# Weights of three key tiles made on VectorE in a cross-attention kernel, lane by lane, and self-attention sums in two banks

## The reference

```python
x = x + _L0_attn_ref(_layernorm(x), L0_attn_Wqvk, L0_attn_Wo)
x = x + _L0_xattn_ref(_layernorm(x), ctx_768, Wq, bq, Wk, bk, Wv, bv, Wo, bo)
x = x + _L0_ffn_ref(_layernorm(x), router_w, router_b, W1, b1, W2, b2)
# cross attention: 16 heads of 8 channels, scale 8 ** -0.5
attn = softmax(einsum('bhqd,bhkd->bhqk', q, k) * scale)
x = einsum('bhqk,bhkd->bqhd', attn, v).reshape(B, Nq, Cq) @ Wo + bo
```

## Time and profile before

| | |
|---|---|
| time, median of three runs | 1010.72 us |
| profiled execution, time | 1012.52 us |
| its span, first to last instruction | 1010.6 us |
| TensorE matmul busy | 878.2 us (87%), 6128 |
| ScalarE busy | 868.4 us (86%), 664 |
| VectorE busy | 178.0 us (18%), 537 |
| mean granted TensorE clock | 0.976 of 2.4 GHz |
| L696, exponentials, ScalarE | 784.3 us, 520 |
| L1341, sums of cross attention | 422.6 us, 3200 matmul records |
| L1311, scores | 266.1 us, 1792 matmul records |

### The profile page before, as it was taken

How to read it: one execution, slowest core, us unless ns; L and a number is a source line. 1 busy time by engine, 2 the same in 40 slices (tenths; PEclk the granted TensorE clock), 3 DMA queues, 4 the chain that set the end, 5 groups by cost and what they waited for, 6 DMA issues and landing times.

```text
span 1010.6 us, 14927 instructions
## 1 busy us (share of the span) xinstructions
PE 878.2 (87%) x6128; PEld 257.8 (26%) x6128; DVE 178.0 (18%) x537; ACT 868.4 (86%) x664; POOL 8.6 (1%) x33
## 2 busy tenths in 40 slices
PE   6978888999888888888899888888888888899997
PEld 4552222222111111111112211111111111134443
DVE  6755644320000000000003000000000000043212
ACT  4656888999999999999999999999999999943332
POOL 3000000000000000000000000000000000000000
PEclk9985999999999999999999999999998999999999
DMA  4251006511112111111221111111221000020200
GB/s 142 105 188 38 1 2 117 182 32 32 35 38 51 43 34 32 32 35 34 42 55 33 36 32 35 35 32 41 41 46 35 3 1 1 1 85 1 84 11 10
DMA packets 19717, 46.32 MB, mean 46 GB/s; under 512 B 6210, under 2 KB 9388, under 8 KB 19132
## 3 DMA queue, kind: packets, MB, share of 16 engines
q1 hardware_dynamic: 19644, 45.31, 17.9%
HBM read 38.18 MB, written 7.11 MB: 45 GB/s over the span
## 4 chain that ended last, share of the span: by engine, by line
PE 34%; issue 31%; ACT 31%; DVE 3%; DMA 0%; ACTq 0%; DVEq 0%
ACT probs L696 31%; PE psum L1341 10%; PE psum L1311 6%; PE psum L1561 5%; PE psum L1573 5%; PE psum L1210 1%; PE psum L1244 1%; PE psum L1458 1%; DVE turned L914 1%; PE psum L1248 1%; PE psum L1337 1%; PE psum L1231 0%; PE psum L1444 0%; PE psum L1194 0%; DVE xn L787 0%
## 5 line engine op out<-in xcount | busy, mean ns | idle before, releaser
L696 ACT ACTIVATE probs<-psum 128x1536 f32<-128x1536 f32 (+1 forms) x520 | 784.3, 1777 | 36.9 <-PE psum L1311 24.6
L1341 PE MATMUL psum<-probs,v_ctx 128*9 128x512 f32 x3200 | 422.6, 600 | 3.1 <-DVE turned L914 2.7
L1311 PE MATMUL psum<-q_all,k_ring 32*128 32x512 f32 (+1 forms) x1792 | 266.1, 496 | 106.1 <-ACT probs L696 100.4
L1311 PEld LDWEIGHTS psum<-q_all,k_ring 32*128 32x128 f32 x1792 | 103.7, 186 | 503.1 <-ACT probs L696 452.1
L914 DVE STREAM_TRANSPOSE turned<-psum 128x512 f32<-128x512 f32 x16 | 11.5, 717 | 626.2 <-PE psum L1337 609.0
L748 ACT ACTIVATE probs<-psum,b_sb 128x512 f32<-128x512 f32 x64 | 44.0, 687 | 71.9 <-PE psum L1561 71.8
L1341 PEld LDWEIGHTS psum<-probs,v_ctx 128*9 128x9 f32 x3200 | 47.6, 88 | 104.7 <-issue 97.7
L1561 PE MATMUL psum<-xnT,w_region 128*128 128x512 f32 x128 | 65.3, 594 | 1.9 <-issue 1.9
L1573 PE MATMUL psum<-probs,ctx_region 128*128 128x512 f32 x128 | 65.0, 592 | 0.0
L1341 PE MATMUL psum<-probs,v_self 128*9 128x512 f32 (+3 forms) x384 | 43.3, 553 | 2.9 <-DVE turned L914 1.7
L1573 PEld LDWEIGHTS psum<-probs,ctx_region 128*128 128x128 f32 x128 | 24.3, 190 | 30.6 <-issue 30.6
(11 more groups left out here) (144 smaller groups left out, 251.3 us busy)
## 6 DMA issues: line engine op xcount, KB each, us to landing
k_ring<-kc_parts SPq DMA_DIRECT2D x256, 52.0 KB
k_ring<-kc_parts SPq DMA_DIRECT2D x256, 48.0 KB
kc_parts<-kparts_bc SPq DMA_DIRECT2D x8, 512.0 KB, 2.8
probs<-gate_rows SPq DMA_DIRECT2D x4, 1024.0 KB, 6.0
kc_parts<-probs SPq DMA_DIRECT2D x4, 512.0 KB, 2.8
w_region<-in_L_ffn_W SPq DMA_DIRECT2D x1, 2048.0 KB, 13.3
ctx_region<-in_ctx SPq DMA_DIRECT2D x1, 768.0 KB, 7.8
ctx_region<-in_ctx SPq DMA_DIRECT2D x1, 672.0 KB, 6.3
```

The source lines that it names most:

```text
L696: act.activation(probs[:, slot:slot + w, :], psum[:, at:at + w, :], ACT.Exp, scale=SC[ph]).then_inc(L[ph]["exp_done"], 1)
L1311: mm = pe.matmul(into[:, col:col + n_q], keys, q_all[rows, g, hf * HALF + q0:hf * HALF + q0 + n_q], start=True, stop=True)
L1341: mm = pe.matmul(into[:, q0:q0 + w], v_all[:, h, t, :], probs[:, place(ph, at)[1], col:col + w], start=first, stop=last)
```

## The change

**A plan with tiles for VectorE.** In units 1, 2, 3, 5, 6 and 7 the tiles 0, 13 and 26 are taken out of ScalarE's list. Their banks (four lanes each, 72 in all) are laid one at a time into bank 3 of every other group of four, beside three of ScalarE's, as soon as ScalarE's list has reached that tile. In unit 1 the lanes of tile 0 stand in groups 67, 71, 75 and 79, those of tile 13 in 83, 87, 91 and 95, those of tile 26 in 99, 103, 107 and 111; the other units have the same spacing. The number of groups is unchanged. The batch of such a tile comes `VECTOR_LAG` = 6 groups behind its last lane: that of tile 0 in turn 85.

**What VectorE does for a lane.** The queries are scaled so that the scores are in powers of two (ScalarE's exponential multiplies with ln 2). VectorE rounds to the nearest integer, takes the rest, builds the power of two from the integer's bits and multiplies it with a polynomial of the rest: eight instructions, each waiting for the one before. The factor in front of the polynomial is multiplied into a copy of the values of the three tiles (`vector_v`, three more instructions before cross attention). The weights lie in four buffers, one per lane, in the space of `v_self` and `w_quads`. TensorE waits before it scores into a bank for the first two of the eight (`taken`), and before a batch for the last (`made`).

**Self attention.** The first half's sums alternate between banks 7 and 6. The mask of diagonal blocks with the same columns in neighbouring slots is one instruction: 53 instead of 128.

**The start.** Layer norm takes both halves at once, with three rounds. The norms of the context are computed within the preparation loop, seven tiles behind it; TensorE reads the branch's condition in the loop, and waits for `outs_cleared` only before its first sums.

```diff
+VECTOR_TILES = (0, 13, 26)
+VECTOR_UNITS = (1, 2, 3, 5, 6, 7)
+VECTOR_LAG = 6
...
+        while scalar:
+            size = 3 if threes > 0 else (4, 3)[n % 2]
...
+            vector = size == 4 and bool(lanes) and lanes[0][2] <= scalar[0][2] and fours % 2 == 0
+            fours += size == 4
+            take = min(size - vector, len(scalar))
+            banks, scalar = scalar[:take], scalar[take:]
+            put(banks + [lanes.pop(0)] if vector else banks, at, vector)
...
+            ready = max(group_of[r, g, t, half] for r in range(LANES))
+            order.append((ready + (VECTOR_LAG if vector else 0), t, vector))
...
+def taken_before(group):
+
+    return sum(CROSS_GROUPS[n][3] for n in range(1 + max([m for m in range(group) if meets(1, m, group, 1)], default=-1)))
...
+        vector_p = [v_self[:, :, :, :].rearrange("p h t c -> p (h t c)")[:, r * HALF:(r + 1) * HALF] for r in range(2)] + \
+            [w_quads[:, :, :, :, :, :].rearrange("p w g r j d -> p (w g r j d)")[:, r * HALF:(r + 1) * HALF] for r in range(2)]
...
+                    scores = bank(GROUPS[1][groups[r]][1] + scalar_banks(1, groups[r]))
+                    dve.wait_ge(L[1]["qk_done"], groups[r] + 1)
+                    dve.tensor_scalar(vector_n, scores, ROUND, None, ALU.add).then_inc(L[1]["rounded"], 1)
+                    dve.wait_ge(L[1]["rounded"], n + 1)
+                    dve.scalar_tensor_tensor(vector_u, vector_n, ROUND, scores,
+                                             ALU.subtract, ALU.subtract).then_inc(L[1]["taken"], 1)
+                    dve.wait_ge(L[1]["taken"], n + 1)
+
+                    powered(dve.tensor_scalar(vector_n.bitcast(I32), vector_n, 127.0 - ROUND, 2.0 ** 23, ALU.add, ALU.mult))
+                    if tile and r == 0:
+                        unit_before, _, _, t_before, _ = VECTOR_WORK[tile - 1]
+                        dve.wait_ge(L[1]["pv_batches"], vector_batch(unit_before, t_before))
+                    weights = vector_p[r]
+                    powered(dve.scalar_tensor_tensor(weights, vector_u, POWERS[4], vector_u, ALU.add, ALU.mult))
+                    for c in (3, 2, 1):
+                        powered(dve.scalar_tensor_tensor(weights, weights, POWERS[c], vector_u, ALU.add, ALU.mult))
+                    dve.scalar_tensor_tensor(weights, weights, POWERS[0], vector_n, ALU.add, ALU.mult)\
+                        .then_inc(L[1]["made"], 1)
+                    dve.wait_ge(L[1]["made"], n + 1)
+
                 while n < len(ends):
+                    if ph == 1:
+                        for tile, work in enumerate(VECTOR_WORK):
+                            if work[0] == n:
+                                for r in range(LANES):
+                                    vector_lane(tile, r)
                     unit(n)
...
-                for _ in range(4):
+                for _ in range(3):
...
-            pe.wait_ge(s["outs_cleared"], 1)
...
-                        held = before_in(ph, group + 2, 2)
+                        held = before_in(ph, group + 2, 1)
                         if held > group:
                             pe.wait_ge(L[ph]["exp_done"], held + 1)
+                        if ph == 1 and taken_before(group + 2):
+                            pe.wait_ge(L[1]["taken"], taken_before(group + 2))
                         score_group(ph, group + 2)
...
+                        if ph == 1 and batches[n][6]:
+                            vector_sums += 1
+                            pe.wait_ge(L[1]["made"], vector_sums * LANES)
                         sum_batch(n)
```

More of the change, by code:

```diff
@@ L8 @@
+import math
 from contextlib import ExitStack
@@ L137, with score_groups @@
[L137 to L141, removed]
+    units = [(half, g) for half in range(NHALF) for g in range(QUADS)]
+    return [(half, g, [(t, n in VECTOR_UNITS and t in VECTOR_TILES) for t in range(KT)])
+            for n, (half, g) in enumerate(units)]
+def score_groups(banks, sizes, slot):
+    groups, at = [], 0
+    while at < len(banks):
+        w = min(sizes[len(groups) % 2], len(banks) - at)
+        slot = slot if slot + w <= SLOTS else 0
+        groups.append((banks[at:at + w], len(groups) % 2 * sizes[0], slot, False))
+        slot, at = slot + w, at + w
+    return groups, slot
@@ L148, in n_groups, with scalar_banks, slot_of, meets @@
     return len(GROUPS[ph])
-def place(ph, at):
-    first, _, psum, slot = GROUPS[ph][GROUP_OF[ph][at]]
-    return psum + at - first, slot + at - first
+def scalar_banks(ph, group):
+    here, _, _, vector = GROUPS[ph][group]
+    return len(here) - vector
+def slot_of(bank):
+    group = CROSS_GROUP_OF[bank]
+    here, _, slot, _ = CROSS_GROUPS[group]
+    return slot + here.index(bank)
+def meets(ph, a, b, which):
+    size = (lambda n: len(GROUPS[ph][n][0])) if which == 1 else (lambda n: scalar_banks(ph, n))
+    return GROUPS[ph][a][which] < GROUPS[ph][b][which] + size(b) and GROUPS[ph][b][which] < GROUPS[ph][a][which] + size(a)
@@ L157, in before_in @@
 def before_in(ph, group, which):
[L159 to L162, removed]
+    return next((n for n in range(group - 1, -1, -1) if meets(ph, n, group, which)), None)
+def taken_before(group):
+    return sum(CROSS_GROUPS[n][3] for n in range(1 + max([m for m in range(group) if meets(1, m, group, 1)], default=-1)))
 def batch_ready(ph, n):
-    places = PLANS[ph][1][n][4] or PLANS[ph][1][n - 1][4]
@@ L182, in diagonals, with sum_bank @@
+def sum_bank(ph, half, g):
+    return OUT_BANK - (ph == 0 and half == 0) * (g % 2)
 def diagonals(group):
-    first, w, _, _ = GROUPS[0][group]
-    return [(place(0, at)[1], col) for at in range(first, first + w) for _, t, half, q0, n, col in PLANS[0][0][at][1]
-            if half * HALF + q0 == t * P]
+    here, _, slot, _ = GROUPS[0][group]
+    blocks = sorted((col, slot + i) for i, (_, pieces) in enumerate(here)
+                    for _, t, half, q0, n, col in pieces if half * HALF + q0 == t * P)
+    runs = []
+    for col, at in blocks:
+        if runs and runs[-1][2] == col and sum(runs[-1][:2]) == at:
+            runs[-1][1] += 1
+        else:
+            runs.append([at, 1, col])
+    return runs
```

242 lines of the change are left out of this document (164 added, 78 removed).

## The result

The changed kernel takes 1088.66 us (median of four runs, 1085.7 to 1090.44), the kernel before 1011.81 beside it: a ratio of 1.0754, with a 95% interval of 1.072 to 1.0789. It is slower, by 77 us. The profiled execution has a span of 1088.7 us and a mean granted clock of 0.934; before they were 1010.6 and 0.976.

The account below looks back on a forecast made before the run. ScalarE's exponentials set the pace in cross attention. From the profiled 1012.5 us: -31 saving, +47 tile changes, +18 unit starts, +9 small waits, +20 clock, -4 other edits gave 1071.5, median 1070, range 1040 to 1100.

Parts of the forecast that it names:

- small waits: Vector units after each stall: the next lanes start behind and catch nothing up, 1.5 us a unit, 9 us.
- other edits: Head, context norms, masks, sums in two banks, small scalings: together -4 us, between -7 and 0.
- 72 banks off ScalarE: Cross attention: 72 banks of exponentials at 0.43 us leave ScalarE, 31 us less.
- six unit starts: First lane waits behind the previous unit's transpose, reciprocal and product: ScalarE idle 2.8 to 3 us each, 18 us.
- twelve changes of tile: Lane 0's fourth instruction waits for the previous tile's sums: ScalarE idle 3.9 us each, 47 us.
- main account: Whole kernel: slower, 1070 us, own range 1058 to 1082, chance 0.48.
- (a): Rival: a lane takes 6.2 us, so VectorE paces each cycle of 14 banks; 1086 us, chance 0.15.
- (c): Rival: the lower clock costs its full 2.2 us at each stall; 1090 us, chance 0.13.
- The saving: Cross attention cycle of four groups: ScalarE needs 5.8 us instead of 6.2, TensorE 5.2, so TensorE would follow.
- The clock: TensorE falls to its lower clock after most of the 18 stalls, 1.1 us each, 20 us.
- The lane: VectorE's eight instructions for a lane: 5.8 us, as long as its cycle, with the conversion at 0.71.
- Rival (d): Faster: stalls hidden by something unseen, or lanes finish well ahead; 976 us, chance 0.07.

Follow-up runs that it names:

- e5: Changed kernel with no unit giving tiles to VectorE, and score groups running on across units: 1002.7 us, 0.9899 of the kernel before.
- e11: Changed kernel with sums two groups behind the last lane, first lane in the third group of four, score groups running on across units: 982.19 us.
- e8: Changed kernel with sums two groups behind the last lane instead of six, and a unit's first lane in the third group of four: 995.79 us.
- e9: Changed kernel with one number changed, sums of a vector tile two groups behind its last lane instead of six: 1029.12 us.
- e3_buf6: Changed kernel with six weight buffers in rotation instead of four, places of lanes and sums unchanged: 1028.68 us.
- e7_busy: Changed kernel with four unread matmuls of 128x512 at each of the 18 places where TensorE waits long for VectorE: 1064.22 us.
- e1_none: Changed kernel with no unit giving tiles to VectorE, only the other edits left: 1017.64 us, 1.0078 times the kernel before.
- e6_both_seam: Changed kernel with first lane in the third group of four, six weight buffers, and score groups running on across units: 989.2 us.

## Why the prediction was right, and where it was not

The forecast was 1070 us, "slower", with 1040 to 1100 around it. The experiments make a ladder from one kernel to the other, so each term can be held against its measured step. A step holds what it does to the clock, so I spread the 29 us of the forecast for small waits and clock over the 18 stalls.

| step | runs | forecast, us | measured, us |
|---|---|---|---|
| other edits, without the seam | before to e5 | -4 | -8.5 |
| 72 banks off ScalarE, no stalls | e5 to e11 | -31 | -20.5 |
| seam between units | e11 to e8 | none | +13.6 |
| six unit starts | e8 to e9 | 18 + 10 | +33.3 |
| twelve changes of tile | e9 to the changed kernel | 47 + 19 | +59.5 |
| sum | | +59 | +77.4 |

The measured steps run from the kernel before to the changed one, so they add up to the whole by construction (77.4 from the 1011.2 of the kernel before that stood beside e5, 76.9 from the result's 1011.8) and their sum checks nothing. They were measured in this order; in another the seam would have another share (14.9 without lanes, 3.3 and 19.7 in the two other pairs).

The forecast was 1070 and the result is 18.7 above it. It lies outside the range given for the main account, 1058 to 1082, and by the number alone nearer to rivals (a), 1086, and (c), 1090; it is the experiments that put both aside. The wide range of 1040 to 1100 held although a term was missing. That is partly luck: the other edits and the changes of tile came out 11 us better than forecast, the other three steps 29 us worse. The units with lanes were to take 98 to 102 us; they took 103.2, 104.6, 103.6, 104.7, 104.9 and 99.1.

**Change of tile: right,** in place, number and mechanism. Forecast: VectorE stands 5.4 us and ScalarE 3.9, 12 times; profile: 5.67 to 5.79, and 3.95 to 4.25. e3_buf6 and e9_lag2 remove the wait in two ways and gain 60.0 and 59.5. My 66 was a little high.

**Unit start: right in kind, small in size.** 2.8 to 3 us forecast, 4.15 measured in unit 1 and 3.95 in unit 2 (2.78 in unit 5, 5.79 in unit 7). The term that failed is the time from the last exponential of a unit to its transpose: 2.4 us forecast, from 257.1 to 259.54. Here is the end of unit 1 after the change, where the last exponential is done at 352.06 us (348.79 + 3.27 in ScalarE's timeline):

```profile
352.16 0.70 PE L1482 MATMUL psum<-q_all,k_ring 32*128 32x512 f32 x4 [1.39 <-ACT probs L811]
...
352.89 2.87 ACT L811 ACTIVATE probs<-psum 128x1536 f32<-128x1536 f32 x2 [0.83 <-PE psum L1482]
...
355.06 1.04 PE L1520 MATMUL psum<-ptail,v_ctx 128*9 128x512 f32 x8
356.24 0.72 DVE L1030 STREAM_TRANSPOSE turned<-psum 128x512 f32<-128x512 f32 x1 [19.25 <-PE psum L1520]
```

At the seam the scores of the new unit's first group come behind the last exponential, and then a batch, more scores, another batch and the tail. So the transpose comes 4.2 us behind, 1.7 later than forecast. ScalarE's two groups also begin 0.83 late and end 0.7 later than forecast, and the stall grows by the rest, 1.0 us.

**The seam: missed.** It stands in the diff as a loop per unit in place of one list, and I read only its lanes. I took 200 banks a unit as running on. It is the largest single error, 13.6 us: ScalarE's idle time at the borders and, at four of them, the clock lost behind it.

**The saving: the term was too large.** ScalarE's own work fell as forecast: 84.27 us in a unit of e11 against 89.07 in e5, 4.8 of 5.2. But 1.15 us of idle time came in, most of it in two pieces of 0.48. I had TensorE at 5.2 of 5.8 us in a cycle and left it there, though a group with its batch costs it 1.41 and a group of three only 1.34 on ScalarE: in a run of threes it has nothing to spare, and a vector tile's batch comes on top. In e11's timeline of unit 2 both pieces lie directly behind such batches, at 364.53 and 388.31 us; no run takes them away. Between the profiled executions of e5 and e11 the six units save 23.4 us and unit 0 another 2.1, but the stage behind cross attention is 4.7 us longer (124.5 instead of 119.8), with TensorE idle for 3.09 us before its first expert matmul. This last part I did not forecast, and no run shows its cause.

**The clock: right as a cost.** Forecast 20, and 24.4 measured by e7_busy; with the 9 of small waits, which were mostly clock too, the forecast was 29. The mean clock fell to 0.89 to 0.93 in the six units with lanes and stayed 1.00 in unit 4. Between runs of one kernel it does the same: e1_none's span is 1009.7 us at 0.988 and 1020.3 at 0.972. Rival (c), the full cost of 2.2 at each stall, would be 40 us and is too much. The Trainium skill, "TensorE: Matmul & The Clock Gate", section "HAM oscillation — how this bites in real kernels", says that waits which recur in a loop lose the clock at each of them. The trace agrees: the lower level follows each of the 18 stalls, in which TensorE waited 2.99 to 3.93 us.

**The lane: 5.5 us, not 5.8.** The conversion takes 0.43 us where I took 0.71. The rest was right to a hundredth, so rival (a), 6.2, is out. The Trainium skill, "VectorE: DVE Perf Modes", section "Mode 2×_2P — use both read ports for one tensor", says that a one-source operation wholly in SBUF gives two results a cycle. The trace agrees: 427 ns, against 692 for the one-source operation of the same size that reads PSUM. It changed little, since the sum was made of places where VectorE waits, not of its speed.

**The other edits** saved 8.5 where I had 4 at most 7: unit 0 ends at 251.07 in e5_none_seam, 259.54 before. The exponentials start 3.9 us earlier in the profile after (2.7 forecast), and the rest lies in self attention and unit 0, where 53 masks instead of 128 and sums in two banks are the edits. Which of them saves it wasn't tried.

Rival (d), faster, is the nearest miss in meaning: it needs an average stall below 1.9 us, and "another order than the one I read". e11_lag2_start_seam is that order. Three small edits decide between 1089 and 982: where a unit's lanes begin, one number for their sums, and score groups that run on across units.

## What to carry to other kernels

When work moves to an engine that is nearly fully used in its cycle (5.5 us of 5.8 here), look for the places where it must wait for its consumer: each of the 18 waits here passed through TensorE's fixed order to ScalarE. Give a buffer back earlier, or start a lane later, before buying more memory: a lag of 2 instead of 6 did what two more buffers did. And when a planner is rewritten, compare its output at the borders, where two groups in the same banks met here seven times, not only where the new feature is.

## What was not expected of the hardware

A stall's price is more than its idle time. After a stall of 3 to 4 us TensorE ran a batch in 1.90 us instead of 1.05, ScalarE lost another 1.1 us once or twice, and four unread matmuls in each of 18 gaps made the kernel 24.4 us faster, though they add work to an engine that is already 85% busy.

The kernel before drops to the lower clock now and then with gaps of only 1.2 us; the fastest variant doesn't do so at all between 240 and 856 us. Two variants with much the same waits of TensorE for ScalarE (e6_both_seam and e11_lag2_start_seam: 55.4 us in both, the longest 1.2 and 1.3) differ by 7 us, and within units 1 to 7 such drops are in the slower one alone; what sets them off stays open.
